# Relative attention with fp32 scores in 32x32 tiles of TensorE and a merged bias band

## The reference

```python
qkv = (x @ w_qkv.T).reshape(B, N, 3, H, hd).transpose(2, 0, 3, 1, 4)
q, k, v = (qkv[0] * scale, qkv[1], qkv[2])
attn = jnp.einsum('bhid,bhjd->bhij', q, k)
rp = clip(j - i, -31, 31) + 31                       # 63 buckets
attn = attn + take_along_axis(q @ rpe_k_table, rp)            # bias of the queries
attn = attn + swapaxes(take_along_axis((k * scale) @ rpe_q_table, rp))   # bias of the keys
attn = jax.nn.softmax(attn, axis=-1)
out = jnp.einsum('bhij,bhjd->bhid', attn, v)
S = segment_sum(attn over j by bucket rp)            # the "bins"
out = out + jnp.einsum('inbh,hnd->bhid', S, rpe_v_table)
return out.reshape(B, N, C) @ w_proj.T + b_proj
```

## Time and profile before

| | |
|---|---|
| median of 3 runs | 4701.89 us |
| the profiled execution | 4712.8 us, its span 4711.0 us |
| granted clock of TensorE, mean | 0.926 |
| busy over the span | PE 3972.3, DVE 2794.0, ACT 1958.2, POOL 1120.2 us |
| DMA over the span | 522.09 MB, 111 GB/s |

### The profile page before, as it was taken

The page is one execution under the profiler, slowest core; times in us unless marked ns, Lnnn a source line. Parts: engine busy times, 40 slices in busy tenths (PEclk is TensorE's granted clock), DMA queues, the critical chain, the costliest instruction groups (busy, mean ns, idle before and its releaser), DMA issues. The chain is left out here.

```text
span 4711.0 us, 85627 instructions
## 1 busy us (share of the span) xinstructions
PE 3972.3 (84%) x27720; PEld 3159.9 (67%) x27720; DVE 2794.0 (59%) x6190; ACT 1958.2 (42%) x4694; POOL 1120.2 (24%) x969
## 2 busy tenths in 40 slices
PE   4888888888888759579999389888899869489998
PEld 3656565665566558468888267777777768478887
DVE  3667666666666546865555445545455456855554
ACT  1555455555555313034444144444444423044443
POOL 1344334343434100023333100000000000033432
PEclk9999899999999879789999599999999969699999
DMA  4556455464656351034433400000000042054442
GB/s 178 177 193 211 159 179 195 166 204 157 204 174 205 124 189 69 18 130 119 127 111 81 142 12 11 15 13 14 14 13 14 10 151 81 4 165 111 127 118 49
DMA packets 348863, 522.09 MB, mean 111 GB/s; under 512 B 106192, under 2 KB 256592, under 8 KB 334928
## 3 DMA queue, kind: packets, MB, share of 16 engines
q1 hardware_dynamic: 188752, 416.74, 24.8%
q10 hardware_dynamic: 135168, 67.13, 5.0%
q0 software_dynamic: 24576, 33.57, 4.2%
HBM read 303.44 MB, written 213.91 MB: 110 GB/s over the span
## 5 line engine op out<-in xcount | busy, mean ns | idle before, releaser
L2040 POOL TENSOR_TENSOR a_win<-a_win,a_tri 128x512 f32<-128x512 f32 x256 | 326.4, 1288 | 226.0 <-DMA a_win<-band 218.2
L1993 ACT ACTIVATE a_prob<-a_ps_s,a_low 128x512 f32<-128x512 f32 x512 | 349.3, 693 | 12.7 <-DVE a_low L2136 12.7
L2136 DVE TENSOR_REDUCE a_low<-a_ps_s 128x2 f32<-128x1024 f32 x256 | 313.4, 1224 | 8.8
L1915 PE MATMUL a_ps_p<-a_ident,a_prob 128*128 128x128 f32 x2048 | 305.8, 284 | 0.6 <-ACT a_probT L2011 0.3
L2034 POOL TENSOR_TENSOR a_tri<-a_lower,a_edge 128x512 f32<-128x512 f32 x128 | 133.4, 1042 | 710.1 <-ACT a_edge L1962 696.1
L1915 PEld LDWEIGHTS a_ps_p<-a_ident,a_prob 128*128 128x128 f32 x2048 | 245.4, 147 | 67.0 <-issue 51.0
L2146 DVE CUSTOM_DVE_ANT_0 a_junk<-a_prob,a_lower 128x128 f32<-128x128 f32 x512 | 255.2, 525 | 17.2 <-DVE a_o L2107 17.2
L1907 PE MATMUL a_ps_s<-a_ident,a_win 128*128 128x128 f32 x1024 | 261.6, 339 | 0.0
L2142 DVE COPY a_probT<-a_ps_p 128x512 f32<-128x512 f32 x256 | 174.8, 683 | 138.7 <-PE a_ps_p L1915 138.6
L1492 POOL TENSOR_TENSOR b_rrms<-b_ms,b_minus_half 128x2 f32<-128x2 f32 x32 | 22.6, 707 | 961.1 <-DVE b_ms L1522 961.1
L1476 ACT ACTIVATE b_prob<-b_score,b_low 128x256 f32<-128x256 f32 (+1 forms) x512 | 240.6, 473 | 24.7 <-PE b_ps_p L1418 23.8
(11 more groups left out here) (381 smaller groups left out, 11696.3 us busy)
## 6 DMA issues: line engine op xcount, KB each, us to landing
band<-a_band SPq DMA_DIRECT2D x256, 384.0 KB, 4.6
a_win<-band SPq DMA_DIRECT2D x256, 384.0 KB, 5.3
prob<-a_prob ACTq DMA_DIRECT2D x128, 384.0 KB, 3.7
xnT<-n_xnT SPq DMA_DIRECT2D x32, 512.0 KB, 3.0
a_bins<-prob ACTq DMA_DIRECT2D x128, 128.0 KB, 3.7
fe_gT<-in_WgT SPq DMA_DIRECT2D x16, 1024.0 KB, 4.9
fe_uT<-in_WuT SPq DMA_DIRECT2D x16, 1024.0 KB, 5.3
fe_dT<-in_WdT SPq DMA_DIRECT2D x16, 1024.0 KB, 5.0
```

What stands on the lines that cost most here:

```text
L1915: mm = nc.tensor.transpose(ps_p[k % 2][:, c * P:(c + 1) * P], prob[:, t % 2, h, 32 + c * P:32 + (c + 1) * P], ident[:, :])
L1993: nc.scalar.activation(prob[:, t % 2, h, 32:32 + T], ps_s[k % 2][:, r, :], ACT.Exp, bias=low[:, k % 2, r:r + 1], accum_out=rsum[:, p, t, h ...
L2040: nc.gpsimd.tensor_tensor(square, square, tri[:, d, :, :], ALU.add).then_inc(win_ready, 1)
L2136: nc.vector.reduce_max(low[:, k % 2, :], both[:, :, :], AX.X, negate=True).then_inc(maxed, 1)
```

## The change

The two orders of `relative_stage` become four lists, one each for the steps' order on TensorE, ScalarE and VectorE and one for the start. `LEAD` says how many units ahead of its use a step is done: q and v three, k and the key bias's first tables two, its sums and the band one. The probabilities' transposes now belong to the tile before, the values and `lower` to the tile two before.

- The split to float32r, the stacks and the eight band products go. q, k_low and k_up stay in fp32, with the far-end bias in spare rows of each head's 32; `k_low` is for keys left of a block of 32 queries, `k_up` for the others. A score step is eight (tile 0: seven) pairs of products of 32 rows by 32 columns, each pair two heads.
- The bias of both sides is brought to one band before it becomes windows. Five tables (`g_pos`, `g_low`, `g_up` from k_low; `s_neg`, `s_pos` from q) give with one 128x512 product each. The keys' part goes to memory as `gbias` (two writes a unit), comes back skewed as `shifted` (eight reads a unit), is added by VectorE to `summed`, transposed into `band`, completed by GpSimd (`sums`), and written and read skewed as windows: four writes of 252 B pieces and four reads a unit.
- v has a column of ones, so that the row sum comes out of the values; the exponentials have no accumulator read. For keys under the diagonal in the tile's own square GpSimd masks the transposed probabilities with a triangle (`mask`), and TensorE adds v_step times that (`lower`).
- The setup on VectorE builds the tables, masks, scales and shifts from the same inputs.

```diff
-                            if t:
-                                nc.tensor.matmul(bank[:, 0:t * P], q_tile, k_stack[r, p, 0, k % 2, 0:t * P], start=True, stop=False)
-                            nc.tensor.matmul(bank[:, t * P:], q_tile, k_stack[r, p, 1, k % 2, t * P:], start=(t == 0), stop=False)
...
-                            mm = nc.tensor.matmul(bank[:, t * P:(t + 1) * P], win[:, p, K, t, h, 32:160], ident[:, :], start=False, stop=True)
...
+LEAD = {"q": 3, "v": 3, "k": 2, "g_pos": 2, "g_low": 2, "g_up": 2, "s_neg": 1, "s_pos": 1, "band": 1, "bins_T": -1, "bins": -1, "out": -1}
...
+RELATIVE_PROLOGUE = [
+    ("q", 0, 0), ("k", 0, 0), ("g_pos", 0, 0), ("g_low", 0, 0), ("g_up", 0, 0), ("v", 0, 0),
+    ("q", 1, 0), ("k", 1, 0), ("s_neg", 0, 0), ("s_pos", 0, 0), ("band", 0, 0), ("band", 0, 1),
+    ("g_pos", 1, 0), ("g_low", 1, 0), ("g_up", 1, 0), ("q", 2, 0), ("v", 1, 0), ("v", 2, 0),
+]
...
 RELATIVE_ORDER = [
+    ("scores", 0), ("k", 0), ("scores", 1), ("probs_T", 0), ("probs_T", 1), ("values", 0), ("s_neg", 0), ("probs_T", 2), ("lower", 0), ("probs_T", 3),
...
+RELATIVE_VECTOR_ORDER = [
+    ("max", 0), ("max", 1), ("s_neg", 0), ("probs_T", 3), ("o", 0),
...
+            def key_bias(b, g):
+
+                u = NG * b + g
+                for i, kind in ((1, "g_pos"), (0, "g_up")):
+
+                    if not (isinstance(u, int) and u == 0):
+                        hold(sp, shifted_in[i], 16 * HG * u, held)
+                    hold(sp, emptied, section(b, g, kind) + 1, held)
+                    sp.dma_start(scratch["shift"][i][:, 32:32 + T], gbias[:, i, :]).then_inc(gbias_out[i], 16)
+                for i in (1, 0):
...
+                    hold(sp, gbias_out[i], 16 * u + 16, held)
+                    for h in range(HG):
...
+                        sp.dma_start(shifted[32 * h:32 * h + 32, i, :], skewed).then_inc(shifted_in[i], 16)
...
+            def unit(b, g):
+                if has_step(b, g, "band", 0):
+                    windows(*unit_after(b, g, 1))
...
+                if has_step(b, g, "k", 0):
+                    key_bias(*unit_after(b, g, 2))
...
+            def scores(b, g, t, pair):
+                n = tile_number(b, g, t)
+                hold(pe, emptied, section(b, g, "k") + 1, held)
+                if not (isinstance(n, int) and n == 0):
+                    hold(pe, exped, HG * n - HG + 2 * pair + 2, held)
+                for up in range(2):
+                    for i in range(4):
+                        own = t * P + 32 * i
+                        keys, cols = ((k_low, slice(0, own)), (k_up, slice(own, T)))[up]
+                        if own == 0 and not up:
+                            continue
+                        for h in (2 * pair, 2 * pair + 1):
+                            r = slice(32 * h, 32 * h + 32)
+                            last = nc.tensor.matmul(ps_s[h // 2][32 * i:32 * i + 32, h % 2, cols], q[r, g, own:own + 32], keys[r, g, cols], start=True, stop=True)
+                last.then_inc(scored, 1)
...
+            def lower(b, g, t):
+                pe.wait_ge(masked, tile_number(b, g, t) + 1)
+                for h in range(HG):
+                    last = nc.tensor.matmul(ps_o[32 * h:32 * h + 32, t * P:(t + 1) * P], v_step[:, g, h, :], below[:, t % 2, h, :],
+                                            start=False, stop=True, skip_group_check=True)
+                last.then_inc(lowered, 1)
...
+                    nc.scalar.activation(prob[:, t % 2, h, 32:32 + T], ps_s[pair][:, r, :], ACT.Exp, bias=low[:, h:h + 1]).then_inc(exped, 1)
...
+                nc.gpsimd.tensor_tensor(below[:, t % 2, :, :], probT[:, t % 2, :, t * P:(t + 1) * P],
+                                        upper[:, :].unsqueeze(1).to_broadcast([P, HG, P]), ALU.mult).then_inc(masked, 1)
...
+                elif kind in ("s_neg", "s_pos"):
+                    i = 0 if kind == "s_neg" else 1
+                    dve.wait_ge(shifted_in[i], 16 * HG * (NG * b + g) + 16 * HG)
+                    dve.wait_ge(filled, n + 1)
+                    last = nc.vector.tensor_tensor(summed[:, i, :], ps_w[:, :], shifted[:, i, :], ALU.add)
```

More of the change, by code:

```diff
@@ L1653, in relative_stage @@
[L1653 to L1666, removed]
@@ new lines, in relative_stage @@
+        xT = s.sb("xT", [P, KC, T])
+        q = s.sb("q", [P, NG, T])
+        k_low = s.sb("k_low", [P, NG, T])
+        k_up = s.sb("k_up", [P, NG, T])
+        v = s.sb("v", [P, NG, 2, NT, HG, 32])
+        shifted = s.sb("shifted", [P, 2, T])
+        summed = s.sb("summed", [P, 2, T])
+        gbias = s.sb("gbias", [P, 2, T])
+        band = s.sb("band", [P, NT, HG, XB])
+        same = s.sb("same", [P, 2, HG, 32])
+        win = s.sb("win", [P, 2, NT, HG, WIN])
+        low = s.sb("low", [P, HG])
@@ L1709, in relative_stage @@
+        bins_in = [s.sem(f"bins_in{i}") for i in range(2)]
         o_taken = s.sem("o_taken")
[L1710 to L1714, removed]
@@ L1715, in relative_stage @@
-        block = ctx.enter_context(s.programs())
[L1717 to L1731, removed]
+        o_out = [s.sem(f"o_out{i}") for i in range(2)]
@@ L1749, in first_unit @@
[L1749 to L1765, removed]
[L1766 to L1767 removed]
+                unit(B - 1, g)
@@ new lines, in empty @@
+            def empty(kind, b, g):
+                act.wait_ge(filled, section(b, g, kind) + 1)
+                if kind == "q":
+                    last = nc.scalar.activation(q[:, g, :], ps_w[:, :], ACT.Identity, bias=shift[:, 0:1], scale=scale[:, 0:1])
+                elif kind == "k":
+                    for i, keys in enumerate((k_low, k_up)):
+                        last = nc.scalar.activation(keys[:, g, :], ps_w[:, :], ACT.Identity, bias=shift[:, 2 + i:3 + i], scale=scale[:, 2 + i:3 + i])
+                else:
+                    i = 1 if kind == "g_pos" else 0
+                    if not (isinstance(b, int) and NG * b + g == 0):
+                        act.wait_ge(gbias_out[i], 16 * (NG * b + g))
+                    last = nc.scalar.copy(gbias[:, i, :], ps_w[:, :])
@@ new lines, in _ @@
+            for kind, u, k in RELATIVE_PROLOGUE:
+                if kind in ("v", "g_up", "s_neg", "s_pos"):
+                    empty(kind, 0, u, ch)
+            units(nc.vector, unit)
+            ch = Chain(dve, chain, SETUP + 9 * NG * B - 1)
+            turned("probs_T", HG * (NT - 1) + 1, B - 1, NG - 1, ch)
+            turned("probs_T", HG * (NT - 1) + 3, B - 1, NG - 1, ch)
+            take(B - 1, NG - 1)
+            empty("bins", B - 1, NG - 1, ch)
+            turned("out", 0, B - 1, NG - 1, ch)
```

720 lines of the change are left out of this document (416 added, 304 removed).

## The result

The changed kernel takes 4949.90 us (median of 4 runs, 4929.47 to 4953.93) against 4699.59 us (4 runs, 4694.70 to 4708.14): a ratio of 1.0522, 95% interval 1.0489 to 1.0555. The prediction was 4442 us, with a chance of 0.88 for faster. The change went the other way: 508 us above the forecast and 324 above the 4625 where its range ended.

The account below looks back on a forecast made before the run. TensorE was taken to bound the stage, busy 41.5 of 47.0 us a unit. New stage end 153 + 32 x 38.0 - 22 + 15 = 1362 us against 1622, so 4712.8 - 260 = 4453, as median 4442; 8 in 10 within 4346 to 4625.

Parts of the forecast that it names:

- TensorE's work: TensorE's busy time in the relative stage: 41.5 us a unit becomes 38.6, with score steps of 1.15 us.
- Rivals 2 and 3: TensorE's score tiles run only two (5114 us, chance 0.06) or four at once (4687 us, chance 0.07), not eight.
- rival 2: Score tiles on TensorE run only two at a time: 3.6 us a step, 21 us more a unit, 5114 us; chance 0.06.
- Other engines, setup, end: Per unit VectorE 24.5 us, ScalarE 23, GpSimd 8, all beside TensorE; first scores at 153 us; 15 us after the last unit.
- The waits: TensorE's waits for bins' copy, split and stacks go: 119.3 us, 3.7 of 5.5 idle us a unit; other engines' work lies alongside.
- What is late next: Key bias's way through memory on SP's one queue: 23.0 us once round, with TensorE's walk 37.1, 37.9 with half clock.
- The clock: TensorE's granted clock in the stage: mean 0.95 kept from before, about a tenth of the time at half speed.
- The ring round memory: Key bias through memory and back to TensorE's next `g_pos`: 37.9 us a unit, as long as TensorE's own work.
- rival 1: Key bias's loop through memory outlasts TensorE's work: 43.7 us, 5.7 a unit over forecast, 4624 us; chance 0.12.
- The slower case: Chance 0.10 that the whole kernel gets slower; score tiles only two at a time would give 5114 us.
- an unforeseen wait: The remaining chance, 0.03, for a wait in the kernel not named elsewhere; no place or size given.

Follow-up runs that it names:

- key bias first: As both, with SP's two `gbias` writes put ahead of the windows and the skewed reads behind them: 4456.18 us, ratio 0.9483 to the kernel before.
- `o` late: Changed kernel with VectorE's copy of finished outputs moved behind `probs_T` 7, one tile later: 4633.72 us, ratio 0.9856 to the kernel before.
- both: Changed kernel with VectorE's output copy behind `probs_T` 7 and SP's xT load ahead of the windows: 4528.60 us, ratio 0.9629 to the kernel before.

## Why the prediction was wrong

The sum over medians, from the changed kernel to key bias first: 4949.9 - 316 (`o`) - 105 (xT, between `o` late and both) - 72 (key bias) = 4456 us, 14 from the 4442 predicted. The prediction priced a kernel whose queues do not stand in each other's way. That only 14 are left is in part luck. Against the 4453 forecast for a profiled run, that of key bias first (4449.2) has its first scores 11 us early, its first 28 units 18 us over, its last four 4 over and the rest of the program 14 under (3075.1 against 3088.7); and it lies 7 under its own median, where the prediction took it 11 over.

1. **TensorE's work: right.** A score step was taken as 1.15 us and is 1.02 from start to start (920.86 to 921.88), with all eight tiles beside each other: one after another they would take 7.3 us. Rivals 2 and 3 (two or four at once) are out. The order of the starts shows it too. In tile 0 the program issues all 12 passes of `k_low` ahead of those of `k_up`, and the trace of the changed kernel has

```profile
912.44 0.30 PE L2009 MATMUL a_ps_s<-a_k_low,a_q 32*32 32x32 f32 x6
912.48 0.62 PE L2009 MATMUL a_ps_s<-a_k_up,a_q 32*32 32x512 f32 x2
912.50 0.20 PE L2009 MATMUL a_ps_s<-a_k_low,a_q 32*32 32x32 f32 x2
...
912.53 0.29 PE L2009 MATMUL a_ps_s<-a_k_low,a_q 32*32 32x64 f32 x4
```

   so two passes of `k_up` start ahead of six of `k_low`. By the Trainium skill's rule in "TensorE: Matmul & The Clock Gate", "Part 3: Packing small matmuls — row/col tiling", that matmuls start in program order, a step would have been the 3.6 us of rival 2; the trace disagrees with it, the more so as issuing the heads apart changed the time by only 0.4%. TensorE is busy 1160 / 31.9 = 36.4 us a unit in key bias first, 38.6 were forecast; the score steps are 1.0 of the difference, and `lower`, at 0.36 instead of 0.25, is 0.4 the other way. In the changed kernel it is 42.9, of the same work, by the clock.
2. **Other engines, setup, end: right; the start by a wrong clock.** VectorE 24.0 us a unit (24.5), ScalarE 19.6 (23), GpSimd 7.7 (8). TensorE's first projection is at 83.85 us (86) and the first scores at 142.6 (153): the projections and tables between were taken as 65 us at half clock and took 58.8, with a granted clock of 1.00 from 84 to 106 us. The last four units and the end were forecast as 4 x 38 - 22 + 15 = 145 us and take 149 in key bias first (1223.2 to 1372.2).
3. **"The waits" and "What is late next": the step that failed.** The prediction added up the busy time of VectorE, found 24.5 of 38 us, and concluded that its work lies beside TensorE's. It did not walk VectorE's list against TensorE's. `o` in the second tile and the `lower` that it needs, put by TensorE's list at the end of that same tile, are both in the lists; so are maxima 2 and 3 behind `o`. The wait needed no new price: 927.5 - 921.7 follows from the two orders and durations that the prediction had. In place of no wait, TensorE stood 4.95 us in the unit shown and 160 us in all. With the half clock behind these waits it cost 295 to 316 us, shown twice, once by taking it out and once by putting it back.
4. **The same step on SP.** The prediction followed SP's queue for the key bias alone. The load of xT in that queue was never asked about, though it had moved behind the windows and the new `LEAD` of three had moved q, its user, from one unit ahead to three. It cost 105 to 121 us, shown twice.
5. **The clock: mis-sized.** The prediction took a tenth of the time at half clock over from before; it was 36%. The clock is no property of the stage, it follows the waits: 0.82 with all of them, 0.92 and 0.85 with one sort gone, 0.95 with both, 0.98 and 0.99 at the end. For each microsecond that TensorE waited behind `o` the time grew by about 2 (316 / 154); behind xT by about 1.1 (121 / 113); these waits are long and few, 7 in all.
6. **The ring round memory: right in kind, too short.** It was forecast as long as TensorE's work, 37.9 against 38, and so at no cost. It stood in the changed kernel as TensorE's 35.9 us of wait, 1.1 a unit, and in the kernel with both edits as 41.3; taking the writes of `gbias` out of it gave 72 us, 2.3 a unit (3.0 by the units' starts). From the first band write of a unit to the landing of its last read of `shifted` the prediction counted 18.5 us. In the kernel with both edits:

```profile
615.98 2.77 SPq L1887 DMA_DIRECT2D band<-a_band  x4
...
629.97 4.55 SPq L1876 DMA_DIRECT2D a_shifted<-shift  x8
```

   With 2.4 us to land (median) this is 20.9, and 20.2 on average over 29 units. The four window reads took about 4 to 5 us to issue, where 1.6 were counted, and the writes of `gbias` landed in 4.9, where 4.2 were. So rival 1 (5.7 a unit) happened to about half; the window reads landed in 4.9 to 5.0 us, where it wanted 5.3.
7. **The chances.** The slower case rested on one mechanism, slow tiles. 0.03 was left for "an unforeseen wait", in a change that writes the orders of TensorE, ScalarE, VectorE and SP anew. That is where the time went: 316 + 105 of the 508 us, where the range had room for 183.

## What to carry over

Busy time says which engine can bound a stage, not that the others keep out of its way: where a change rewrites the orders by hand, walk each engine's list, and SP's, once through a unit against TensorE's, and ask of each waiting step when its producer stands in the other list and what is queued behind it. Here a wait of TensorE of a few microseconds cost about twice its length (316 us for 154, 72 for 41), since half clock followed it; the seven waits of 16 us cost about their length. A kernel that is slower by a queue's order can be one line from being faster: look at its largest waits before giving up the idea.

## What the runs showed of the hardware

- **Half clock after a short wait.** Windows of the changed kernel before the wait of 4.95 us, after it, and behind that:

```profile
918.00:927.50 9.50, 9.50 (x152) 5.49 (x142) 1.75 (x3) 4.25 (x8) 1.27 (x1) 1.00 0.36 101
933.12:943.36 10.24, 10.24 (x111) 6.10 (x109) 5.18 (x7) 2.68 (x5) 1.26 (x1) 0.50 0.13 41
943.40:952.00 8.60, 8.31 (x102) 5.12 (x102) 4.92 (x7) 3.85 (x8) 3.94 (x5) 1.00 0.15 34
```

  TensorE is busy without a gap in the middle stretch and still runs at 1.2 GHz for 10.24 us. Others were 6.8 us (after a loop's turn) and 13.7 us long. Even a wait of 2.05 us in the kernel with both edits was followed by a table product of 2.07 us instead of 1.13; the granted clock is 1.00 from 585.0 to 594.0 us there and 0.50 from 594.5 to 600.5:

```profile
594.59 2.07 PE L1957 MATMUL a_ps_w<-a_k_low,a_tables 128*128 128x512 f32 x2 [2.05 <-DVE a_summed L2271]
```

- **The turn of a loop.** TensorE stands still there for nothing that the profile shows, about 5 us at each of 5 turns:

```profile
1019.09 0.40 PE L2009 MATMUL a_ps_s<-a_k_low,a_q 32*32 32x32 f32 x6 [5.05 <-issue]
```

  Written out, the same units show no such row, and their starts give 37 us of the gain: 23 of idle time and the half clock behind it. What fills the 5 us stays open.

- **Eight 32x32 tiles.** Two row groups by four column groups, each tile with 512 columns in fp32, take 1.02 us together. Eight products of 512 columns at 0.91 us one after another would take 7.3, about seven times as long.
